# Two products of the second layer from rounded halves instead of native fp32

## What is computed

```
xn = layernorm(x)
q, k, v = heads of xn @ W_qkv;  q, k turned by position;  q = elu(q/4) + 1;  k = elu(k) + 1
kv = sum_t k[t] v[t]^T;  att = (q @ kv) / max(q . sum_t k[t], 1e-6)
xk = mu_k * xn + (1 - mu_k) * xn_prev;  xr likewise with mu_r      # xn_prev: one position earlier
gate = sigmoid(xr @ W_r^T);  act = relu(xk @ W_k^T)^2              # "k product": xk @ W_k^T
out = x + att @ W_out + gate * (act @ W_v^T)                       # "output product": att @ W_out
```

## Time and profile before

| | us |
|---|---|
| three runs | 957.64, 957.75, 958.78 (median 957.75) |
| the profiled execution | 961.03 |
| its span, first to last instruction | 959.4 |
| granted clock of TensorE, mean over the span | 0.986 of full |
| TensorE busy | 904.6 (94%) |
| VectorE busy | 742.6 (77%) |
| ScalarE busy | 581.7 (61%) |
| GpSimd busy | 188.3 (20%) |

### The profile page before, as it was taken

One profiled execution on the slowest core, in us unless ns is written; L12 is line 12 of the kernel. 1 busy time (PEld: TensorE's weight loads), 2 busy tenths in 40 slices (PEclk: granted clock), 3 DMA queues, 4 the chain that ended last, 5 costly groups with the idle time before them and its releaser, 6 DMA issues. The chain is left out here.

```text
span 959.4 us, 18851 instructions
## 1 busy us (share of the span) xinstructions
PE 904.6 (94%) x6533; PEld 842.0 (88%) x6533; DVE 742.6 (77%) x1432; ACT 581.7 (61%) x1131; POOL 188.3 (20%) x208
## 2 busy tenths in 40 slices
PE   3899999899999999999999999989679999898998
PEld 2688999899999999999999999988677887777877
DVE  7677555888888888888888888864758777797764
ACT  3643434566666666666666666655377678477581
POOL 1004776000000000000000000006006154261202
PEclk9999999999999999999999999999879999999999
DMA  7792446686666666666666666604002021030101
GB/s 260 264 311 79 153 153 209 238 311 219 219 219 219 219 219 219 219 219 219 219 219 219 219 219 219 208 33 103 3 1 71 18 75 58 1 105 27 44 1 44
DMA packets 103813, 150.36 MB, mean 157 GB/s; under 512 B 8480, under 2 KB 86880, under 8 KB 103648
## 3 DMA queue, kind: packets, MB, share of 16 engines
q1 hardware_dynamic: 94592, 123.13, 38.7%
q0 software_dynamic: 9184, 26.75, 8.0%
HBM read 112.63 MB, written 37.22 MB: 156 GB/s over the span
## 5 line engine op out<-in xcount | busy, mean ns | idle before, releaser
L950 ACT ACTIVATE h<-ps,b1T 128x256 f32<-128x256 f32 x312 | 129.5, 466 | 141.0 <-PE ps L885 141.0
L883 PE MATMUL ps<-w2h,hh 128*128 128x256 f32 x624 | 179.9, 288 | 1.0 <-DVE hl L1004 0.9
L883 PE MATMUL ps<-xTh,w1h 128*128 128x256 f32 x624 | 177.6, 285 | 1.4 <-DVE xTl L987 1.4
L884 PE MATMUL ps<-xTl,w1h 128*128 128x256 f32 x624 | 177.3, 284 | 0.0
L885 PE MATMUL ps<-xTh,w1l 128*128 128x256 f32 x624 | 177.2, 284 | 0.0
L885 PE MATMUL ps<-w2h,hl 128*128 128x256 f32 x624 | 176.9, 283 | 0.0
L884 PE MATMUL ps<-w2l,hh 128*128 128x256 f32 x624 | 176.7, 283 | 0.0
L1004 DVE TENSOR_TENSOR hl<-h,hh 128x512 fp32r<-128x512 f32 x156 | 107.6, 690 | 51.6 <-ACT hh L954 51.5
L883 PEld LDWEIGHTS ps<-xTh,w1h 128*128 128x128 f32 x624 | 120.5, 193 | 1.6 <-DVE xTl L987 1.6
L883 PEld LDWEIGHTS ps<-w2h,hh 128*128 128x128 f32 x624 | 119.8, 192 | 1.6 <-DVE hl L1004 1.6
L884 PEld LDWEIGHTS ps<-xTl,w1h 128*128 128x128 f32 x624 | 120.6, 193 | 0.0
(11 more groups left out here) (272 smaller groups left out, 2134.1 us busy)
## 6 DMA issues: line engine op xcount, KB each, us to landing
raw<-in_L_ffn_W SPq DMA_DIRECT2D x40, 1024.0 KB, 8.4
raw_odd<-in_L_ffn_W SPq DMA_DIRECT2D x38, 1024.0 KB, 8.4
dispatched<-shared SPq DMA_DIRECT2D x1, 9984.0 KB, 34.8
rows<-dispatched SPq DMA_DIRECT2D x39, 256.0 KB, 6.0
expert_out<-y POOLq DMA_DIRECT2D x38, 256.0 KB, 6.9
xn_rows<-raw SPq DMA_DIRECT2D x4, 1024.0 KB, 5.3
rows<-xn_rows SPq DMA_DIRECT2D x32, 128.0 KB, 2.1
x_acc<-in_L_attn_x SPq DMA_DIRECT2D x3, 1024.0 KB, 9.3
```

Of the source, the lines that this page charges most:

```text
L883: pe.matmul(out, ah, bh, start=start, stop=False, skip_group_check=True)
L884: pe.matmul(out, ah, bl, start=False, stop=False, skip_group_check=True)
L950: op = act.activation(h32[:, k, :], ps[:, q, (k % 2) * M:(k % 2 + 1) * M], ACT.Relu, bias=s.b1T[:, ds(e * HC + k, 1)])
```

## The change

The k product and the output product are made of halves. ScalarE makes the hi halves of both weights once, and of xk in every batch, after `features(0)`; the copy of the turned att out of PSUM becomes its hi half. VectorE makes the lo halves: of the weights once, of xk after `turn_by_position(1)`, of the turned att after `divide(2)` and `divide(3)`. TensorE waits for the lo halves. The halves lie where xrT, act_k, gate and att lie, so ScalarE's `scaled` for xrT waits for the last output product, and the wait for `final` (GpSimd's additions of the batch before) moves from ahead of the gates to ahead of the hi half of xk. v1 moves, so its column of ones is written once layer 0's attention is over. The diff, cut to its core:

```diff
@@ -1056,16 +1056,21 @@ combine_and_layer1, tiles
-        xkT, xrT = sb("xkT", [P, DC, T]), sb("xrT", [P, DC, T])
+        xkT = sb("xkT", [P, DC, T])
         feat = sb("feat", [P, BT, 2 * D])
-        act_k, gate = sb("act_k", [P, DC, T]), sb("gate", [P, BT, D])
-        oT, att = sb("oT", [P, DC, T]), sb("att", [P, BT, D])
+
+        with ExitStack() as shares_with_halves:
+            xrT, act_k, gate, att = (shares_with_halves.enter_context(nc.sbuf_tensor(n, [P, 8 * D], F32)) for n in (
+                "xrT", "act_k", "gate", "att"))
...
+        oTl, oTh, xkh, xkl = (sb(n, [P, DC, T], F32R) for n in ("oTl", "oTh", "xkh", "xkl"))
+        v1 = sb("v1", [P, BT, DC, P + 1])
...
+        wkh, wkl = sb("wkh", [P, DC, D], F32R), sb("wkl", [P, DC, D], F32R)
+        wouth, woutl = sb("wouth", [P, DC, D], F32R), sb("woutl", [P, DC, D], F32R)
@@ -1192,19 +1201,20 @@ gpsimd
-            pool.memset(v1[:, :, :, P:P + 1], 1.0).then_inc(const_ready, 1)
...
             for i in range(1, BT):
                 gather(pool, s, expert_out, 0, i)
+            pool.wait_ge(attended, ATTENDED + BT + 2)
+            pool.memset(v1[:, :, :, P:P + 1], 1.0).then_inc(const_ready, 1)
@@ -1374,14 +1384,16 @@ tensor
-                pe.wait_ge(k_mixed, b + 1)
+                pe.wait_ge(wk_lo, 1)
+                pe.wait_ge(xk_lo, b + 1)
                 pe.wait_ge(qkv_out, NG * b + 2)
                 for n in range(4):
                     m, h = n // 2, n % 2
                     if n == 2:
                         pe.wait_ge(qkv_out, NG * b + 3)
-                    product(ps[:, n, :], lambda c: wT[:, 1, c, tile_of(m)], lambda c: xkT[:, c, half_of(h)]
-                            ).then_inc(k_mm, 1)
+                    product_of_parts(ps[:, n, :], lambda c: wkh[:, c, tile_of(m)], lambda c: wkl[:, c, tile_of(m)],
+                                     lambda c: xkh[:, c, half_of(h)], lambda c: xkl[:, c, half_of(h)]
+                                     ).then_inc(k_mm, 1)
@@ -1430,7 +1442,7 @@ tensor, turn_attention
                     if h:
-                        pe.wait_ge(oT_ready, 4 * b + 2)
+                        pe.wait_ge(oT_lo, 4 * b + 2)
@@ -1438,11 +1450,13 @@ tensor, project_out
-                    pe.wait_ge(oT_ready, 4 * b + 2 * (h + 1))
+                    pe.wait_ge(wout_lo, 1)
+                    pe.wait_ge(oT_lo, 4 * b + 2 * (h + 1))
                     for n in (2 * h, 2 * h + 1):
                         for j in range(2):
-                            mm = product(ps[:, 4 + n, j * D:(j + 1) * D], lambda c: oT[:, c, tile_of(2 * n + j)],
-                                         lambda c: wout[:, c, :])
+                            mm = product_of_parts(ps[:, 4 + n, j * D:(j + 1) * D], lambda c: oTh[:, c, tile_of(2 * n + j)],
+                                                  lambda c: oTl[:, c, tile_of(2 * n + j)],
+                                                  lambda c: wouth[:, c, :], lambda c: woutl[:, c, :])
@@ -1491,9 +1505,11 @@ scalar, scaled
                 for dst, m, done in ((xkT, 1, k_scaled), (xrT, 0, r_scaled)):
+                    if m == 0 and not first:
+                        act.wait_ge(out_mm, NG * b)
@@ -1543,11 +1559,14 @@ scalar
             act.wait_ge(loaded, 16 * LOADS)
+            act.wait_ge(weights_ready, 1)
+            act.activation(wkh[:, :, :], wT[:, 1], ACT.Copy).then_inc(wk_hi, 1)
+            act.activation(wouth[:, :, :], wout[:, :, :], ACT.Copy).then_inc(wout_hi, 1)
@@ -1573,6 +1592,13 @@ scalar, body
                     if n > 0:
                         features(n - 1)
+                    if n == 1:
+                        act.wait_ge(k_mixed, b + 1)
+                        if not first:
+                            act.wait_ge(final, NG * b)
+                        for c in range(DC):
+                            op = act.activation(xkh[:, c, :], xkT[:, c, :], ACT.Copy)
+                        op.then_inc(xk_hi, 1)
@@ -1590,8 +1616,6 @@ scalar, body
-                if not first:
-                    act.wait_ge(final, NG * b)
@@ -1609,7 +1633,7 @@ scalar, body
-                    act.activation(oT[:, c, h * HB:(h + 1) * HB], ps[:, 2 + c, :], ACT.Copy).then_inc(oT_ready, 1)
+                    act.activation(oTh[:, c, h * HB:(h + 1) * HB], ps[:, 2 + c, :], ACT.Copy).then_inc(oT_ready, 1)
@@ -1765,6 +1789,11 @@ vector, body
                 for n in range(1, NG):
                     turn_by_position(n)
+                    if n == 1:
+                        dve.wait_ge(xk_hi, b + 1)
+                        for c in range(DC):
+                            op = V.tensor_tensor(xkl[:, c, :], xkT[:, c, :], xkh[:, c, :].bitcast(F32), ALU.subtract)
+                        op.then_inc(xk_lo, 1)
                     feature(n - 1)
@@ -1806,8 +1835,17 @@ vector, body
+
+                def turned_att_lo(h):
+                    for c in range(DC):
+                        dve.wait_ge(oT_ready, 4 * b + 2 * h + c + 1)
+                        at = (slice(None), c, slice(h * HB, (h + 1) * HB))
+                        V.tensor_tensor(oTl[at], ps[:, 2 + c, :], oTh[at].bitcast(F32), ALU.subtract).then_inc(oT_lo, 1)
+
                 divide(2)
+                turned_att_lo(0)
                 divide(3)
+                turned_att_lo(1)
@@ -1823,6 +1861,10 @@ vector
             dve.wait_ge(const_ready, 6)
+            dve.wait_ge(wk_hi, 1)
+            V.tensor_tensor(wkl[:, :, :], wT[:, 1], wkh[:, :, :].bitcast(F32), ALU.subtract).then_inc(wk_lo, 1)
+            dve.wait_ge(wout_hi, 1)
+            V.tensor_tensor(woutl[:, :, :], wout[:, :, :], wouth[:, :, :].bitcast(F32), ALU.subtract).then_inc(wout_lo, 1)

```

More of the change, by code:

```diff
@@ L1058, in combine_and_layer1 @@
             pTh, pTl = parts("pT_last_", [P, 2, BT, P])
-        xkT, xrT = sb("xkT", [P, DC, T]), sb("xrT", [P, DC, T])
+        xkT = sb("xkT", [P, DC, T])
         feat = sb("feat", [P, BT, 2 * D])
-        act_k, gate = sb("act_k", [P, DC, T]), sb("gate", [P, BT, D])
-        oT, att = sb("oT", [P, DC, T]), sb("att", [P, BT, D])
+        with ExitStack() as shares_with_halves:
+            xrT, act_k, gate, att = (shares_with_halves.enter_context(nc.sbuf_tensor(n, [P, 8 * D], F32)) for n in (
+                "xrT", "act_k", "gate", "att"))
+        xrT, act_k = (a[:, :].rearrange("p (c t) -> p c t", c=DC) for a in (xrT, act_k))
+        gate, att = (a[:, :].rearrange("p (i d) -> p i d", d=D) for a in (gate, att))
+        oTl, oTh, xkh, xkl = (sb(n, [P, DC, T], F32R) for n in ("oTl", "oTh", "xkh", "xkl"))
+        v1 = sb("v1", [P, BT, DC, P + 1])
         prob = qk[:, :, :, :].rearrange("p u j e -> p u (j e)")
@@ L1067, in combine_and_layer1 @@
         rot, straight = (s.shared[:, n, :].rearrange("p (u j d) -> p u j d", u=2, j=2) for n in range(2))
-        v1 = sb("v1", [P, BT, DC, P + 1])
         qT = xkT
@@ L1087, in combine_and_layer1 @@
         turned, xnT_ready, mu_ready = sem("turned1"), sem("xnT_ready1"), sem("mu_ready")
+        wk_hi, wk_lo, wout_hi, wout_lo, xk_hi, xk_lo, oT_lo = (sem(n) for n in (
+            "wk_hi", "wk_lo", "wout_hi", "wout_lo", "xk_hi", "xk_lo", "oT_lo"))
         k_scaled, r_scaled, k_mixed, r_mixed = sem("k_scaled"), sem("r_scaled"), sem("k_mixed"), sem("r_mixed")
@@ L1194, in _ @@
             pool.memset(xnT[:, :, 0:1], 0.0).then_inc(const_ready, 1)
-            pool.memset(v1[:, :, :, P:P + 1], 1.0).then_inc(const_ready, 1)
             heads = same_head[:, :].rearrange("p (h f) -> p h f", f=HD)
-            pool.wait_ge(const_ready, 3)
+            pool.wait_ge(const_ready, 2)
             pool.affine_select(out=heads, in_=heads, compare_op=ALU.is_ge, fill=0.0, base=0,
                                pattern=[[-HD, HP], [0, HD]], channel_multiplier=1).then_inc(const_ready, 1)
-            pool.wait_ge(const_ready, 4)
+            pool.wait_ge(const_ready, 3)
             pool.affine_select(out=heads, in_=heads, compare_op=ALU.is_gt, fill=0.0, base=HD,
                                pattern=[[HD, HP], [0, HD]], channel_multiplier=-1).then_inc(const_ready, 1)
-            pool.wait_ge(const_ready, 5)
+            pool.wait_ge(const_ready, 4)
             pool.tensor_copy(head_of[:, :], heads[:, :, 0]).then_inc(const_ready, 1)
@@ L1492, in turned_out, with scaled @@
                     act.activation(xh[:, c, tokens], xnT[:, c, at], ACT.Copy).then_inc(xh_ready, 1)
-            def scaled(b):
+            def scaled(b, first):
                 act.wait_ge(xnT_ready, all_turned(b))
                 for dst, m, done in ((xkT, 1, k_scaled), (xrT, 0, r_scaled)):
+                    if m == 0 and not first:
+                        act.wait_ge(out_mm, NG * b)
                     for c in range(DC):
@@ L1545, in _ @@
                 if a == 5:
-                    act.wait_ge(const_ready, 3)
+                    act.wait_ge(const_ready, 2)
                     turned_out(0, 0)
@@ L1562, in body @@
                     act.wait_ge(nd_mm, NG * b)
-                scaled(b)
```

(1 more changed line is left out.)

## The result

The changed kernel takes 977.21 us (median; 974.87 to 978.43) where the kernel before, run beside it, takes 958.26: a ratio of 1.0198, 95% interval 1.0171 to 1.0224, or 19.0 us more. The forecast was 975.2, in a range of 968.5 to 982.

A forecast was written before the change was run, and what follows sets the result against it. The prediction took VectorE and ScalarE in alternation, not TensorE, to bound the kernel. Fronts 13.9, tails 2.7 and displaced work 0.9 made 17.5 us, added to 957.75 for 975.2 us, in a range of 968.5 to 982.

The forecast's parts named there:

- The bound: Layer 1: VectorE and ScalarE in alternation set the time, not TensorE, though TensorE is busy 94% of the span.
- TensorE's saving: K product 5.6 us for 6.86, half an output product 2.83 for 3.45; 10.0 us of TensorE time over four batches.
- The fronts: From mix to gates: making xk's halves delays batches 0 to 3 by 2.4, 4.0, 4.0 and 3.5 us, together 13.9.
- The tails: Output products at batch ends wait for lo halves of the turned att: 0.9 + 0.2 + 0.9 + 0.7 = 2.7 us.
- displaced work: At three batch boundaries, VectorE's later additions make GpSimd's additions meet VectorE's next work: 0.3 us each, 0.9 together.
- (a): Rival for the whole kernel: TensorE is the bound and making halves is hidden; 10.0 us less, 947.8 us; chance 4%.
- (b): Rival at the fronts: ScalarE's hi half of xk is hidden, each front 2.0 us less; 967.2 us; chance 10%.
- (c): Rival on TensorE's clock: new waits bring half clock, a slow kv product counting perhaps 2 us in three batches; 981; 12%.
- A sign that the prediction called wrong: Behind TensorE's new waits: a half-clock stretch longer than 4 us would show the forecast wrong.
- (d): Rival for the whole kernel: savings and costs balance by chance, leaving the time within 0.2% (1.9 us); chance 2%.
- the +0.7: In the tails: about 0.7 us more each if products of halves were no faster than native ones, 979.7 us in all.
- At nothing: Terms put at no cost: weights' halves before batch 0's first turn by position (1.3 us if uncovered), moved waits, v1's memset.

The follow-up runs named there:

- lo_twice: The changed kernel with VectorE's lo half of xk made twice, one after the other; 987.7 us, ratio 1.0309 to the kernel before.
- native_k_waiting: The changed kernel with native k product matmuls again, its halves still made and waited for; 979.0 us, ratio 1.0224 to the kernel before.
- free_halves: The changed kernel without making halves of xk or lo halves of the turned att; its products read other halves and compute something else; 952.6 us.
- k_only: The changed kernel with the output product native again, so only the k product is made of halves; 973.9 us, ratio 1.0151 to the kernel before.
- out_only: The changed kernel with the k product native again, so only the output product is made of halves; 962.3 us, ratio 1.0053 to the kernel before.
- adds_first: The changed kernel with the second two lo halves of the turned att behind VectorE's first two additions into x; 976.8 us.
- halves_tuned: The changed kernel with xk's hi half earlier, all relus ahead of features(3), and the turned att's second lo halves behind two additions into x; 965.9 us.
- hi_early: The changed kernel with ScalarE's hi half of xk made after the copies of pair 0, not after features(0); 972.1 us.
- relu_first_before: The kernel before with all four relus of a batch ahead of features(3) on ScalarE; 953.7 us, ratio 0.9948 to the kernel before.

## Why the prediction was right, point by point

**The bound.** Right, and tested from both sides: VectorE's time at the front counts in full (`lo_twice`), TensorE's time in the k product doesn't in batches 0 to 2 and does in batch 3 (`native_k_waiting`), and all of its saving together is worth about half (`free_halves`). VectorE is 5.2 us busier in batch 1, not near 4: the prediction's own prices, 2.36 for xk and 2.5 for the turned att, come to 4.9.

**TensorE's saving.** 5.54 and 2.94 us measured for 5.6 and 2.83. Of the 0.11 more on half an output product 0.07 is its slower start behind a wait, the rest its pace of 0.120 us a matmul.

**The fronts.** Forecast 2.4 + 4.0 + 4.0 + 3.5 = 13.9. From the traces, mix to gate is 31.25 in batches 1 and 2 against 27.4, so 3.86 and 3.85, and in batch 3 the kv product comes 3.4 us later. Batch 0 needs a word. In the two traces its front is even 0.44 us shorter than before, since the profiled execution of the kernel before ran its first qkv product at reduced clock. Before, then after, by stretch (the clock is the third number from the end):

```profile
713.00:720.00 7.00, 6.88 (x26) 5.90 (x27) 6.02 (x7) 2.17 (x4) 0.00 (x0) 0.62 0.00 0
```

```profile
711.80:718.80 7.00, 6.94 (x39) 6.08 (x40) 6.97 (x9) 5.13 (x9) 1.51 (x1) 1.00 0.00 0
```

That is the main reason why the two profiled executions are only 15.9 us apart (961.03 and 976.93), where the medians are 19.0 apart. `free_halves`, whose first qkv product ran at full clock and whose other engines have the work of before but for the weights' halves, is the fairer comparison. Mix and gates, the changed kernel and then `free_halves`:

```profile
714.13 2.48 DVE L1755 SCALAR_TENSOR_TENSOR xkT<-xnT,rest_of_mu,xkT 128x1024 f32<-128x1024 f32 x2
744.13 2.06 ACT L1621 ACTIVATE gate<-ps 128x512 f32<-128x512 f32 x4
```

```profile
713.07 2.48 DVE L1750 SCALAR_TENSOR_TENSOR xkT<-xnT,rest_of_mu,xkT 128x1024 f32<-128x1024 f32 x2
740.25 2.07 ACT L1616 ACTIVATE gate<-ps 128x512 f32<-128x512 f32 x4
```

30.0 us against 27.2, so 2.8 for the 2.4 forecast. Fronts: 2.8 + 3.9 + 3.9 + 3.4 = 14.0, and `k_only` cost 14.5 by the runs.

**The tails.** Forecast 2.7, and 0.9 for displaced work. Measured from the first turn of att to the next mix: 1.36 more in batches 0 and 2, 1.76 in batch 1 and, to the last addition, 1.0 in batch 3: 5.5; `out_only` cost 5.1 by the runs. Three terms of the sum were off. project_out(0) is 1.53 - 0.51 = 1.0 later, not 0.8: the wait was 0.1 longer and the saving 0.1 smaller. The second tail was put at one lo half (0.7) less 0.62: it is 0.92 less 0.62 and 0.04 more by the next mix, 0.34 instead of 0.1, because the two lo halves run one after the other (1.29) and the first can start only when the first copy ends. In batch 1, I counted on the half clock of before as cover; the changed kernel ran its own output product there at half clock for 4.97 us instead of 2.94. Those 1.76 us belong to this execution: from the first turn of att in batch 1 to the next mix it is 19.6 us in the changed kernel, `adds_first` and `halves_tuned`, whose output product ran slow, and 17.5 to 17.6 in `hi_early`, `native_k_waiting` and `lo_twice`. With native products it is 17.80 in the kernel before, partly at half clock, and 16.50 in `relu_first_before`. And the 0.9 for displaced work was 0. So 3.6 were forecast and 5.5 found: the tails were 2.8 us too low, and 0.9 for work that cost nothing made up for a third of it by luck.

**The sum.** 14.0 + 5.5 = 19.5 by these distances, 19.0 measured (16.4 to 21.5 by the interval), 17.5 forecast. The mechanism is the forecast one, and most of what was missing lies in the tails, above all that of batch 1.

**The rivals.** (a) is out by `free_halves`. (b) is what `hi_early` does. (c) happened in its mild form: the k product ran slow in batches 1 and 3 (7.17 us) and not in batch 2; the gates came as late in any case, so it was covered, in batch 3 just; the kv product ran at full clock, so the 6 us never came. The Trainium skill's page "TensorE: Matmul & The Clock Gate" (section "HAM oscillation — how this bites in real kernels") has every group behind a wait start cold in its example; here two of three k products did. A sign that the prediction called wrong did appear, a half-clock stretch of 6.8 us in batch 1, from 829.8 on. It began before TensorE's new wait (0.66 us, up to 832.01) and after one of 1.64 us that the kernel before has as well. In (d), 979.7 needs the +0.7 six or seven times, and the prediction doesn't say at which of the eight half products.

**At nothing.** The memset of v1 (0.13 us) and the waits for `out_mm` and `final` stayed hidden. The weights' halves did not, wholly. Their cover was the 2.62 us that VectorE idled before the first turn by position, which came with a first qkv product at reduced clock; at full clock it is gone:

```profile
712.92 0.69 DVE L1865 TENSOR_TENSOR wkl<-wT,wkh 128x512 fp32r<-128x512 f32 x1
713.53 0.68 DVE L1867 TENSOR_TENSOR woutl<-wout,wouth 128x512 fp32r<-128x512 f32 x1
718.92 1.22 DVE L1765 TENSOR_TENSOR shared<-qk,cos 128x1024 f32<-128x1024 f32 x1
```

Mix (714.13) starts right behind them. `k_only` makes only the first of the two, and from the first qkv matmul to the gates it takes 31.71 us, where the changed kernel takes 32.27: some 0.6 us that the forecast had at nothing. The distances above start at mix and don't hold it.

## What to carry to other kernels

A product made of halves is paid for by the engines that make the halves; before counting matmul columns, find where those engines' queues are full and who waits behind them. An engine at 94% need not be the bound: follow the chain, look for the thread with no gap in it, and test it by adding work there. And where two engines alternate, moving one's work into a gap it already has (four relus here) may be worth as much as faster matmuls: `relu_first_before` gained about what `free_halves` did.

## What was unexpected of the hardware

The granted clock of TensorE varies between executions of the same program, in short stretches. Ten executions of `out_only` took 960.3 to 970.5 us; the six with a mean granted clock from 0.987 to 0.991 took 960.3 to 962.7, and the three with 0.973 to 0.975 took 968.4 to 970.5. The same wait doesn't always bring one: TensorE idled 2.0 us before the k product in batches 1, 2 and 3 of the changed kernel, and of the three products, by stretch,

```profile
795.56:802.73 7.17, 7.17 (x24) 5.76 (x25) 6.86 (x7) 4.88 (x10) 4.83 (x3) 0.76 0.21 58
864.16:869.71 5.55, 5.55 (x25) 4.61 (x26) 5.34 (x6) 3.29 (x8) 4.74 (x3) 1.00 0.24 71
930.83:938.00 7.17, 7.17 (x25) 5.72 (x25) 6.86 (x7) 4.88 (x10) 0.00 (x0) 0.76 0.00 0
```

the first and the last ran partly at half clock (0.76 in the mean, 7.17 us), the one between them at full clock (5.55). What decided between them no run here shows. Such a stretch, in the first qkv product of the kernel before, is the main reason why one profiled execution of each kernel misstated the difference by 3 us, and why a forecast made against one trace should say which stretches of it ran at which clock.
